# A graph layer's edge walk, from single edge rows in 16 slots to fours of rows in 32 slots

## The chip, the cores and the metric

One NeuronCore of one Trainium2 chip runs the whole program. The metric is the device time of one execution in microseconds (us), the median over several runs.

## What is computed

The reference normalizes 6250 nodes of 256 features, adds to them a mean over graph neighbours and a linear attention, and then a mixture of experts. The part that matters here is the neighbour sum over 100,000 edges, sorted by target node (`dst`); `src` is random.

```python
neigh_sum = jax.ops.segment_sum(input_matrix[src], dst, num_segments=N_NODES)
deg = jax.ops.segment_sum(jnp.ones_like(dst), dst, num_segments=N_NODES)
out = jax.nn.relu(concat([x, neigh_sum / max(deg, 1)]) @ W + b)      # GNN
qkv = rmsnorm(x) @ w_qkv
k = softmax(k, over all nodes); q = softmax(q, per head) * SCALE     # linear attention
out = rmsnorm((q @ (k.T @ v)) @ w_out + b_out) + x
x = x + top2_of_8_experts(layernorm(x))
```

## The kernel before

Nodes lie in 49 tiles of 128. Edges lie in rows of 128; 100,000 edges fill 782 rows, padded to 784. In the first stage layer norm is computed for all tiles, z = xn @ W_neigh is written to DRAM (`z_d`), and tables are made on the chip: for each step the row of edges that it takes (`srcT`, `dstT`) and the tile to which it adds (`acc_at`). A step is one row for one tile; a row that two tiles share has two steps. There are 832 steps in 104 blocks of 8 (`STEP_BLOCK`).

**The walk.** A step is four pieces of work on four engines. POOL gathers 128 rows of z (1 KB each) by an indirect DMA into one of 16 slots: a half of 8 slots is `G`, the other lies in `ring` (a part of `w2s`); line 677. DVE builds a 0/1 matrix S for four steps at once by comparing `iota` with `dstT` (`build_S`, line 1229). PE multiplies S of the step by the gathered rows into one of four PSUM banks (`walk` of the tensor block, line 1684; a product in float32 is two instructions in the profile). DVE adds the bank to the tile's accumulator at an address from a register (line 1245); eight registers are loaded at once at the head of a block (line 1234). The engines wait for one another by counting semaphores: POOL takes a group of four slots again when the four products of 16 steps before are signalled (`p_ready`); PE waits for the group's landing (`g_in`), for S (`s_built`), and for the addition four steps back (`acc_done`). `follow` (line 1673) is a filler product of PE after steps 3, 5 and 7 that nobody reads.

**What runs beside it.** The order of each engine is written out by hand, with hooks called after a given step of a block. Blocks 0 to 47 (here called stage A) carry keys and values of one tile each: ACT normalizes it (743), PE transposes it (1696), ACT copies it (862), SP stores it, PE multiplies (1703), ACT copies keys and values (866), DVE keeps the maximum (`kmax_tile`, 1276). Six blocks carry the context (1302, 885, 1724). The next 49 (stage B) carry the mixing of one tile each: SP loads the transposed tile, PE projects (`qu`, 1745), DVE does the first half of a softmax (`b_q1`, 1326 to 1330), ACT the exponential (893), DVE the second half (`b_q2`, 1334 to 1336), PE transposes q (`turn_q`, 1750), ACT copies it (907), PE multiplies (`mix_out`, 1755), DVE and ACT norm the tile before (`b_o1` 1340, 897 to 902, `b_o2` 1346 to 1349), SP stores it. Stage B also splits the second expert weights into two parts (`split_w2`, 440 and 441), and in tiles 16 to 23 sums bias products (`bfold` 1760, `b_fold` 1364). Then the last blocks run alone, and the router (group by group of up to 6 tiles, loads `load_ub` on SP) and the experts follow.

The hooks of stage B on PE: `qu` before the block, `turn_q` after step 5, `mix_out` after step 7. On DVE: `b_q1` after step 0, `b_o1` of the tile before after 1, `b_q2` after 3, `split_w2` after 5, `b_o2` of the tile before after 6.

The waits of POOL and of PE, in the code:

```python
until(pool, s["p_ready"], step - 2 * STEP_BLOCK + S_GROUP)
...
pe.wait_ge(g_in[half][k // S_GROUP], 16 * S_GROUP * (turn + 1))
pe.wait_ge(s["s_built"], 2 * i + k // S_GROUP + 1)
...
until(pe, s["acc_done"], step - 3)
```

## Time and profile before

| | |
|---|---|
| median of 3 runs (lowest, highest) | 2268.57 us (2268.07, 2277.15) |
| the profiled execution's span | 2267.2 us, 1.4 us below the median; the profile gives no other time of its own |
| PE, DVE, ACT, POOL busy | 74%, 58%, 40%, 52% of the span |
| walk, first gather to last addition | 90.5 to 1360 us |
| bytes moved | 325 MB, 143 GB/s on average |

The profile is one execution. Busy times are per engine; PEld is PE's weight load, which lies beside its products. "Idle before" is the time an engine stood before an instruction, with what ended it; "issue" names no releaser, and "remote" is a signal whose sender the trace doesn't name. The clock is PE's granted clock as a share of 2.4 GHz; 0.5 is 1.2 GHz. Line numbers are those of the kernel before. Tiles called `w2s_lent` and `edge_tabs_lent` are regions lent to several uses; `w2s_lent` is the slots of the second half in line 677.

### The profile page before, as it was taken

What the parts mean: (1) busy time and instruction counts of PE and PEld (TensorE: products, weight loads), DVE (VectorE), ACT (ScalarE), POOL (GpSimd) and SP (SyncE); (2) the same over time, 40 slices, a digit from 0 to 9 for tenths busy, and PEclk for the clock granted to TensorE, in tenths of its full rate; (3) what the DMA queues carried; (4) which work ended last, traced back from release to release, by engine and by line L of the source; (5) the groups of instructions that cost most, each with busy time, mean ns of one, the idle gap of its engine ahead of it and who ended that gap; (6) DMA issues with size and microseconds to landing.
All of it is one profiled execution on the core that took longest, in us unless ns stands there. A gap on an engine that the chain in (4) does not pass through costs nothing. (4 is left out here: it accounts for less than half of the span.)

```text
span 2267.2 us, 34877 instructions
## 1 busy us (share of the span) xinstructions
PE 1666.7 (74%) x9448; PEld 1326.2 (58%) x9449; DVE 1305.5 (58%) x3579; ACT 899.5 (40%) x1840; POOL 1177.1 (52%) x1203
## 2 busy tenths in 40 slices
PE   6656566665756666787666663555999999999997
PEld 5534343443434434434444342443999999999996
DVE  6434343443434557776777667753666666666663
ACT  6501010110110233333444336642666666666663
POOL 3466666666656666666666543663333333333333
PEclk9867777776768877889787885557999999999998
DMA  7433333333333465656666536745565565555554
GB/s 203 122 111 106 100 104 100 103 105 96 103 95 91 149 222 178 195 180 190 184 206 191 181 110 199 257 167 156 122 137 129 128 136 128 133 130 134 132 126 93
DMA packets 193411, 325.02 MB, mean 143 GB/s; under 512 B 34453, under 2 KB 136865, under 8 KB 192286
## 3 DMA queue, kind: packets, MB, share of 16 engines
q0 software_dynamic: 80912, 208.73, 35.0%
q1 hardware_dynamic: 103574, 112.56, 16.2%
q10 hardware_dynamic: 8824, 2.61, 0.6%
q8 instruction: 36, 0.59, 0.1%
q14 instruction: 65, 0.53, 0.1%
HBM read 244.30 MB, written 80.26 MB: 143 GB/s over the span
## 5 line engine op out<-in xcount | busy, mean ns | idle before, releaser
L1245 DVE TENSOR_TENSOR acc_lent<-acc_lent,bank 128x258 f32 x832 | 350.0, 421 | 527.5 <-remote 267.6
L677 POOL DMA_INDIRECT G<-z_d,edge_tabs_lent x416 | 404.3, 972 | 294.2 <-issue 119.6
L677 POOL DMA_INDIRECT w2s_lent<-z_d,edge_tabs_lent x416 | 402.0, 966 | 182.3 <-issue 117.8
L1684 PE MATMUL bank<-G,S_lent 128*128 128x258 f32 x832 | 286.0, 468 | 156.3 <-DVE acc_lent L1245 86.2
L1684 PE MATMUL bank<-w2s_lent 128*128 128x258 f32 x832 | 293.6, 478 | 114.7 <-issue 71.9
L1684 PEld LDWEIGHTS bank<-G,S_lent 128*128 128x128 f32 x832 | 166.8, 226 | 240.6 <-issue 167.7
L1684 PEld LDWEIGHTS bank<-w2s_lent 128*128 128x128 f32 x832 | 171.9, 233 | 203.0 <-issue 139.0
L717 POOL DMA_INDIRECT out_dram<-G,acc_lent x112 | 178.3, 1592 | 201.3 <-DVE G L1572 126.3
L1551 DVE TENSOR_TENSOR acc<-w1s,acc 128x512 fp32r<-128x512 f32 x224 | 155.0, 693 | 204.7 <-ACT acc L995 182.5
L1008 ACT ACTIVATE G<-bank,acc_lent 128x256 f32<-128x256 f32 x448 | 188.0, 471 | 195.6 <-DVE acc L1592 84.7
L1888 PE MATMUL bank<-w2s,acc 128*128 x896 | 261.5, 292 | 1.8 <-DMA edge_tabs<-w2lo_d 1.8
L1865 PE MATMUL bank<-acc 128*128 128x256 f32 x896 | 257.7, 288 | 3.4 <-DVE acc L1559 3.4
L1866 PE MATMUL bank<-acc 128*128 128x256 f32 x896 | 253.3, 283 | 0.0
L1867 PE MATMUL bank<-acc 128*128 128x256 f32 x896 | 253.3, 283 | 0.0
L1890 PE MATMUL bank<-w2s,acc 128*128 x896 | 251.5, 281 | 0.0
L866 ACT ACTIVATE w1s<-bank,r 128x256 f32<-128x256 f32 x49 | 23.2, 474 | 519.0 <-remote 332.6
L1865 PEld LDWEIGHTS bank<-acc 128*128 128x128 f32 x896 | 170.3, 190 | 3.9 <-issue 3.9
L1867 PEld LDWEIGHTS bank<-acc 128*128 128x128 f32 x896 | 170.9, 191 | 0.0
L1888 PEld LDWEIGHTS bank<-w2s,acc 128*128 128x128 f32 x896 | 169.7, 189 | 2.0 <-issue 2.0
L1866 PEld LDWEIGHTS bank<-acc 128*128 128x128 f32 x896 | 170.8, 191 | 0.0
L1890 PEld LDWEIGHTS bank<-w2s,acc 128*128 128x128 f32 x896 | 168.3, 188 | 0.0
L1592 DVE TENSOR_TENSOR acc<-G,acc 128x512 fp32r<-128x512 f32 x224 | 154.3, 689 | 7.0 <-ACT acc L1018 6.9
(294 smaller groups left out, 3134.6 us busy)
## 6 DMA issues: line engine op xcount, KB each, us to landing
S<-w2lo_d POOLq DMA_DIRECT2D x56, 512.0 KB
edge_tabs<-w2lo_d POOLq DMA_DIRECT2D x56, 512.0 KB
acc_lent<-bucket_d SPq DMA_DIRECT2D x56, 266.0 KB, 2.9
bu_d<-w2s_lent SPq DMA_DIRECT2D x98, 128.0 KB
w2s_lent<-bu_d SPq DMA_DIRECT2D x12, 768.0 KB
w1s<-in_L_ffn_W_dram SPq DMA_DIRECT2D x8, 1024.0 KB
w2s_lent<-in_L_ffn_W_dram SPq DMA_DIRECT2D x32, 256.0 KB
w2hi_d<-w2s_lent SPq DMA_DIRECT2D x32, 256.0 KB
```

Of the source, the lines that this page charges most:

```text
L677: pool.indirect_dma_start(out=G_half[half][:, k, 0:D], out_offset=None, in_=z_d[:, :], in_offset=bass.IndirectOffsetOnAxis(ap=srcT[:, step ...
L717: pool.indirect_dma_start(out=out[:, :], out_offset=bass.IndirectOffsetOnAxis(ap=nid[par][:, j:j + 1], axis=0), in_=ys[par][:, j, :], in_o ...
L1008: g = act.activation(raw[q % 2][:, k * MT:(k + 1) * MT], bank[q][:, k * MT:(k + 1) * MT], ACT.Gelu, bias=b1c[1 - par][:, 2 * q + k:2 * q + ...
L1245: dve.tensor_tensor(to, to, bank[k % 4][:, 0:ACCW], ALU.add).then_inc(s["acc_done"], 1)
L1551: dve.tensor_tensor(w1lo[:, :, cols].bitcast(F32R), w1_part(e, q), w1hi[:, :, cols], ALU.subtract).then_inc(s["w1_ready"], 1)
L1592: dve.tensor_tensor(hlo[:, cols].bitcast(F32R), raw[q % 2], hhi[:, cols], ALU.subtract).then_inc(s["h_split"], 1)
L1684: pe.matmul(bank[k % 4][:, 0:ACCW], S_half[half][:, k // S_GROUP, k % S_GROUP, :], G_half[half][:, k, :], start=True, stop=True).then_inc( ...
L1865: pe.matmul(to, hi, x_hi, start=(k == 0), stop=False)
L1866: pe.matmul(to, hi, x_lo, start=False, stop=False)
L1867: m = pe.matmul(to, lo, x_hi, start=False, stop=(k == DC - 1))
L1888: pe.matmul(to[j], hi, w_hi, start=False, stop=False, skip_group_check=True)
L1890: m = pe.matmul(to[j], lo, w_hi, start=False, stop=(c == HC - 1), skip_group_check=True)
```

## The change

The walk goes by turns in place of steps. A turn is one tile with a group of four rows (`QUAD`); there are 196 groups and at most 196 + 48 = 244 turns. The 32 slots (`RING` = 8 groups) all lie in `ring`; each row is gathered once, in order, and a group that two tiles share is used by two turns (or more) from the same slots. PE multiplies the four rows into one bank (start at the first, stop at the last), gives one signal, and issues a filler after every turn. DVE makes one addition a turn and builds S for the turn four ahead. Which slots a turn uses, which group it needs and when a group's slots are free depends on the data: three new tables (`base_at`, `need_at`, `free_at`) beside the accumulator's addresses are read into registers, eight at a time, by PE (two tables), POOL and DVE, and PE and POOL wait on those register values. POOL waits for the landing of group q-2 before it issues group q, and then signals it to PE by `quads_in`.

Stage A has two turns a tile, the context two turns a group, stage B three turns a tile for 37 tiles (`B_LONG`) and two for 12; one turn is left at the end. The tables are made in another way: source rows are transposed straight from the loaded edges, target rows come by two gathers of 128 groups in place of seven gathers of rows, and the accumulator's addresses no longer go through DRAM. Regions move: `w_kv`, `headmask`, `mkT`, `w_outs` to the rest of `G`, others to the end of `w2s`. On SP the load for router group 1 waits for the bias sum, and those for groups 2 and 3 for the last addition.

```diff
-STEPS_J = 7
-STEP_BLOCK = 8
-S_GROUP = 4
+QUAD = 4
+QUADS = EROWS // QUAD
+RING = 8
+IN_FLIGHT = 2
+DEPTH = 4
+REGS = 8
...
-BLOCKS = (EFULL + 1 + (NT - 1) + STEP_BLOCK - 1) // STEP_BLOCK
+TURNS = QUADS + NT - 1
+TURN_COLS = 248
...
+        RING_AT = 6 * D
+        RING_END = RING_AT + RING * QW_RING
+        taken = {"a": 0, "t": NT * KVW, "b": RING_END, "c": LATE}
...
+        S_of = [S[:, 0, :, :], S[:, 1, :, :]] + [G_flat[:, k * QUAD * P:(k + 1) * QUAD * P].rearrange("p (b n) -> p b n", n=P)
+                                                 for k in range(2)]
...
+        def groups_of(t):
+
+            if t < B_LONG:
+                return range(B_FIRST + 3 * t, B_FIRST + 3 * t + 3)
+            first = B_FIRST + 3 * B_LONG + 2 * (t - B_LONG)
+            return range(first, first + 2)
...
             load_ub(0)
+            sp.wait_ge(s["b1_mm"], 1)
             load_ub(1)
...
+            sp.wait_ge(s["acc_done"], TURNS)
             load_ub(2)
             load_ub(3)
...
-                pool.wait_ge(s["ecol_ready"], 1)
-                for j in range(STEPS_J):
-                    pool.indirect_dma_start(out=steps_e[:, j].rearrange("p k e -> p (k e)"), out_offset=None,
-                                            in_=edges_d.rearrange("r k e -> r (k e)"),
-                                            in_offset=bass.IndirectOffsetOnAxis(ap=ecol_i[:, j:j + 1], axis=0)
+                pool.wait_ge(s["qcol_ready"], 1)
+                for c in range(2):
+                    pool.indirect_dma_start(out=steps_i[:, c, :], out_offset=None,
+                                            in_=edges_d.rearrange("k (q r) e -> (k q) (r e)", r=QUAD),
+                                            in_offset=bass.IndirectOffsetOnAxis(ap=qcol_i[:, c:c + 1], axis=0)
...
-            pool.wait_ge(s["tables_ready"], 2)
+            pool.wait_ge(s["tables_ready"], 3)
             z_stored(pool)
-            for step in range(STEP_BLOCK * BLOCKS):
-                half, k = step // STEP_BLOCK % 2, step % STEP_BLOCK
-                if k % S_GROUP == 0:
-                    until(pool, s["p_ready"], step - 2 * STEP_BLOCK + S_GROUP)
-                    stand_alone(pool, s["waits_passed"])
-                pool.indirect_dma_start(out=G_half[half][:, k, 0:D], out_offset=None, in_=z_d[:, :],
-                                        in_offset=bass.IndirectOffsetOnAxis(ap=srcT[:, step:step + 1], axis=0)
-                                        ).then_inc(g_in[half][k // S_GROUP], 16)
+
+            def landed(q):
+
+                pool.wait_ge(g_in[q % IN_FLIGHT], 16 * QUAD * (q // IN_FLIGHT + 1))
+                pool.sem_inc(s["quads_in"], 1)
+            for q in range(QUADS):
+                if q >= RING:
+                    if q % REGS == 0:
+                        _, frees = nc.values_load_multi_w_load_instructions(
+                            rows_i[0:1, free_at + q:free_at + q + REGS], engines=[mybir.EngineType.Pool], min_val=1, max_val=TURNS)
+                    pool.wait_ge(s["p_ready"], frees[q % REGS])
+                if q >= IN_FLIGHT:
+                    landed(q - IN_FLIGHT)
+                for k in range(QUAD):
+                    row = QUAD * q + k
+                    pool.indirect_dma_start(out=ring_rows[:, row % (RING * QUAD), 0:D], out_offset=None, in_=z_d[:, :],
+                                            in_offset=bass.IndirectOffsetOnAxis(ap=srcT[:, row:row + 1], axis=0)
+                                            ).then_inc(g_in[q % IN_FLIGHT], 16)
+            for q in range(QUADS - IN_FLIGHT, QUADS):
+                landed(q)
...
+            def build_S(j):
+
+                dve.tensor_tensor(S_of[j % DEPTH], iota[:, :].rearrange("p (o n) -> p o n", o=1).to_broadcast([P, QUAD, P]),
+                                  dstT[:, QUAD * j:QUAD * (j + 1)].rearrange("p (g o) -> p g o", o=1).to_broadcast([P, QUAD, P]),
                                   ALU.is_equal).then_inc(s["s_built"], 1)
-
-            def walk(i, half, hooks={}):
-                _, places = nc.values_load_multi_w_load_instructions(
-                    acc_at[0:1, ds(STEP_BLOCK * i, STEP_BLOCK)], engines=[mybir.EngineType.DVE], min_val=0, max_val=NT * PAYW,
-                    skip_runtime_bounds_check_because="a count of at most NT tiles, times the width of one")
-                for k in range(STEP_BLOCK):
-                    step = STEP_BLOCK * i + k
-                    if k % S_GROUP == 0:
-                        until(dve, s["p_ready"], step - S_GROUP)
-                        build_S(2 * i + k // S_GROUP + 2, 1 - half, k // S_GROUP)
-                    dve.wait_ge(s["p_ready"], step + 1)
-                    until(dve, s["acc_done"], step)
-                    to = acc_flat[:, ds(places[k], ACCW)]
-                    dve.tensor_tensor(to, to, bank[k % 4][:, 0:ACCW], ALU.add).then_inc(s["acc_done"], 1)
-                    if k in hooks:
-                        hooks[k]()
-            build_S(0, 0, 0)
-            build_S(1, 0, 1)
+            places = {}
+
+            def turn(j):
+
+                if j % REGS == 0:
+                    _, loaded = nc.values_load_multi_w_load_instructions(
+                        rows_i[0:1, place_at + j:place_at + j + REGS], engines=[mybir.EngineType.DVE], min_val=0, max_val=NT * PAYW,
+                        skip_runtime_bounds_check_because="a count of at most NT tiles, times the width of one")
+                    places.update({j + k: v for k, v in enumerate(loaded)})
+                dve.wait_ge(s["p_ready"], j + 1)
+                until(dve, s["acc_done"], j)
+                to = acc_flat[:, ds(places[j], ACCW)]
+                dve.tensor_tensor(to, to, bank[j % DEPTH][:, 0:ACCW], ALU.add).then_inc(s["acc_done"], 1)
+                if j + DEPTH < TURNS:
+                    build_S(j + DEPTH)
+            for j in range(DEPTH):
+                build_S(j)
+            dve.memset(kmax, -3e38)
+            z_stored(dve)
+            dve.memset(ring_rows[:, :, D:ACCW], 1.0).then_inc(s["consts_dve"], 1)
...
+            for i in range(NT - 1):
+                turn(2 * i)
                 if i in late:
-                    hk[3] = late[i]
-                return hk
-            blocks(lambda i, h, turn: walk(i, h, a_hooks(i)), 0, NT - 1)
...
+            for t in range(NT):
+                mine = groups_of(t)
                 e = t - 16
-                hk[4] = lambda: (until(dve, s["bf_evac"], 2 * e), b_fold(e, 0))
-                hk[7] = lambda: b_fold(e, 1)
-                return hk
-            walk(B0, B0 % 2, b_hooks(0, True))
-            for first, end, hooks in ((1, SPLIT_AT + 1, b_hooks), (SPLIT_AT + 1, 16, with_split(b_hooks)), (16, 24, with_split(fold_hooks)),
-                                      (24, SPLIT_END + 1, with_split(b_hooks)), (SPLIT_END + 1, NT, b_hooks)):
-                blocks(lambda i, h, turn: walk(i, h, hooks(i - B0)), B0 + first, B0 + end)
-                if end == 24:
+                turn(mine[0])
+                b_q1(t)
+                if t:
+                    b_o1(t - 1)
+                turn(mine[1])
+                b_q2(t)
+                if 0 <= e < EXPERTS:
+                    until(dve, s["bf_evac"], 2 * e)
+                    b_fold(e, 0)
+                if len(mine) > 2:
+                    turn(mine[2])
+                if SPLIT_AT < t <= SPLIT_END:
+                    split_w2(t - SPLIT_AT - 1)
+                if t:
+                    b_o2(t - 1)
+                if 0 <= e < EXPERTS:
+                    b_fold(e, 1)
...
-            def walk(i, half, turn, hooks={}):
-                if -1 in hooks:
-                    hooks[-1]()
-                for k in range(STEP_BLOCK):
-                    step = STEP_BLOCK * i + k
-                    if k % S_GROUP == 0:
-                        pe.wait_ge(g_in[half][k // S_GROUP], 16 * S_GROUP * (turn + 1))
-                        pe.wait_ge(s["s_built"], 2 * i + k // S_GROUP + 1)
-                    until(pe, s["acc_done"], step - 3)
-                    pe.matmul(bank[k % 4][:, 0:ACCW], S_half[half][:, k // S_GROUP, k % S_GROUP, :], G_half[half][:, k, :], start=True, stop=True).then_inc(s["p_ready"], 1)
-                    if k in (3, 5, 7):
-                        follow()
-                    if k in hooks:
-                        hooks[k]()
-                        if k in (3, 7):
-                            follow()
+            bases, needs = {}, {}
+
+            def turn(j):
+
+                if j % REGS == 0:
+                    _, loaded = nc.values_load_multi_w_load_instructions(
+                        rows_i[0:1, base_at + j:base_at + j + REGS], engines=[mybir.EngineType.PE], min_val=0, max_val=(RING - 1) * QW_RING,
+                        skip_runtime_bounds_check_because="a slot of the ring, times the width of one")
+                    bases.update({j + k: v for k, v in enumerate(loaded)})
+                    _, loaded = nc.values_load_multi_w_load_instructions(
+                        rows_i[0:1, need_at + j:need_at + j + REGS], engines=[mybir.EngineType.PE], min_val=1, max_val=QUADS)
+                    needs.update({j + k: v for k, v in enumerate(loaded)})
+                pe.wait_ge(s["quads_in"], needs[j])
+                pe.wait_ge(s["s_built"], j + 1)
+                until(pe, s["acc_done"], j + 1 - DEPTH)
+                for k in range(QUAD):
+                    rows = ring[:, k * ACCW:(RING - 1) * QW_RING + (k + 1) * ACCW]
+                    m = pe.matmul(bank[j % DEPTH][:, 0:ACCW], S_of[j % DEPTH][:, k, :], rows[:, ds(bases[j], ACCW)],
+                                  start=(k == 0), stop=(k == QUAD - 1))
+                m.then_inc(s["p_ready"], 1)
+                follow()
...
+            for i in range(NT - 1):
+                turn(2 * i)
+                turn_a(i + 1)
+                turn(2 * i + 1)
+                kv(i)
...
+            for t in range(NT):
+                mine = groups_of(t)
                 e = t - 16
-                hk[3] = lambda: bfold(e, 0)
-                hk[6] = lambda: bfold(e, 1)
-                return hk
-            blocks(lambda i, h, turn: walk(i, h, turn, b_hooks(i - B0)), B0, B0 + 16)
-            pe.wait_ge(s["w1_in"], 16 * EXPERTS)
-            blocks(lambda i, h, turn: walk(i, h, turn, fold_hooks(i - B0)), B0 + 16, B0 + 24)
-            pe.wait_ge(s["bf_evac"], 2 * EXPERTS)
-            for c in range(HC):
-                m = pe.matmul(bank[5][:, c * EXPERTS:(c + 1) * EXPERTS], bacc[0:EXPERTS, c * P:(c + 1) * P], ident[0:EXPERTS, 0:EXPERTS],
-                              start=True, stop=True)
-            m.then_inc(s["b1_mm"], 1)
-            follow()
-            blocks(lambda i, h, turn: walk(i, h, turn, b_hooks(i - B0)), B0 + 24, B0 + NT)
-            walk(B0 + NT, (B0 + NT) % 2, (B0 + NT) // 2)
-            blocks(lambda i, h, turn: walk(i, h, turn), B0 + NT + 1, BLOCKS)
-            pe.wait_ge(s["acc_done"], STEP_BLOCK * BLOCKS)
+                if e == 0:
+                    pe.wait_ge(s["w1_in"], 16 * EXPERTS)
+                qu(t)
+                turn(mine[0])
+                if 0 <= e < EXPERTS:
+                    bfold(e, 0)
+                turn(mine[1])
+                turn_q(t)
+                if 0 <= e < EXPERTS:
+                    bfold(e, 1)
+                if len(mine) > 2:
+                    turn(mine[2])
+                mix_out(t)
...
+CTX_FIRST = 2 * (NT - 1)
+B_FIRST = CTX_FIRST + 12
+B_LONG = TURNS - 1 - B_FIRST - 2 * NT
```

## Rows read from the trace of the kernel before

**Rows 1.** Busy time by stretch: length, engines (instructions), clock, DMA share, GB/s.
```profile
0.00:90.50 90.50, 62.98 (x325) 51.46 (x326) 59.42 (x269) 65.99 (x146) 23.02 (x38) 0.98 0.65 177
90.50:669.00 578.50, 359.55 (x1204) 233.94 (x1204) 232.27 (x541) 59.52 (x145) 384.48 (x399) 0.73 0.36 103
669.00:750.00 81.00, 52.03 (x234) 38.04 (x235) 37.87 (x80) 8.31 (x10) 49.80 (x50) 0.77 0.29 86
750.00:1358.50 608.50, 421.88 (x1428) 254.03 (x1426) 418.37 (x1163) 222.10 (x405) 372.05 (x384) 0.82 0.60 183
```

**Rows 2.** Groups on POOL, 90 to 1358: busy and mean; idle before, by releaser.
```profile
L677 POOL DMA_INDIRECT G<-z_d,edge_tabs_lent x416 | 404.3, 972 | 294.2 <-issue 119.6 <-PE bank L1684 79.1 <-remote 69.2
L677 POOL DMA_INDIRECT w2s_lent<-z_d,edge_tabs_lent x416 | 402.0, 966 | 182.3 <-issue 117.8 <-PE bank L1684 41.5 <-remote 23.1
```

**Rows 3.** Timeline of POOL: start, length, instruction, idle before.
```profile
...
515.79 0.94 POOL L677 DMA_INDIRECT G<-z_d,edge_tabs_lent  x1 [0.30 <-issue]
517.04 0.94 POOL L677 DMA_INDIRECT G<-z_d,edge_tabs_lent  x1 [0.30 <-issue]
522.39 0.94 POOL L677 DMA_INDIRECT w2s_lent<-z_d,edge_tabs_lent  x1 [4.41 <-PE bank L1684]
```

**Rows 4.** Waits of DVE, 750 to 1358: total, times, longest.
```profile
DVE acc_lent L1245 <- remote: 86.3, 23, 7.0
```

**Rows 5.** Timeline, 804 to 825: products on PE, an addition on DVE.
```profile
804.44 1.93 PE L1684 MATMUL bank<-G,S_lent 128*128 128x258 f32 x4
...
817.34 1.91 PE L1684 MATMUL bank<-G,S_lent 128*128 128x258 f32 x8
...
824.22 0.42 DVE L1245 TENSOR_TENSOR acc_lent<-acc_lent,bank 128x258 f32 x1 [5.64 <-remote]
```

**Rows 6.** Timeline of DVE, 546.96: tile maximum and build of S.
```profile
546.96 0.29 DVE L1276 TENSOR_TENSOR w2s_lent<-w1s,w2s_lent 128x128 f32<-128x128 f32 x1
547.39 0.69 DVE L1229 TENSOR_TENSOR w2s_lent<-iota,edge_tabs_lent 128x512 f32<-128x512 f32 x1
```

**Rows 7.** Timeline at the first gather and the first product.
```profile
90.53 1.25 POOL L677 DMA_INDIRECT G<-z_d,edge_tabs_lent  x1 [26.29 <-DMA z_d<-w2s_lent]
...
97.39 2.95 PE L1684 MATMUL bank<-G,S_lent 128*128 128x258 f32 x6 [7.45 <-DMA G<-z_d,edge_tabs_lent]
```

**Rows 8.** Timeline between the context and the first mixing product.
```profile
741.86 0.22 PE L1673 MATMUL bank<-ones_b,before 128*128 128x128 bf16 x1
...
747.37 2.92 PE L1745 MATMUL bank<-w2s_lent,xTs 128*128 128x384 f32 x4 [0.46 <-DVE w2s_lent L1316]
```

**Rows 9.** Busy time of line 1684 alone by stretch: PE, PEld, clock.
```profile
90.50:669.00 578.50, 293.39 (x768) 156.75 (x768) 0.73 0.36 103
...
750.00:1358.50 608.50, 249.93 (x800) 161.56 (x799) 0.82 0.60 183
```

**Rows 10.** Timeline of DVE in a mixing tile: the two softmax parts.
```profile
803.29 0.28 DVE L1334 TENSOR_REDUCE small<-w2s_lent 128x4 f32<-128x128 f32 x1
...
803.82 0.29 DVE L1336 TENSOR_TENSOR w2s_lent<-w2s_lent,small 128x128 f32<-128x128 f32 x1
...
824.56 0.34 DVE L1326 TENSOR_SCALAR w2s_lent<-bank,r 128x128 f32<-128x128 f32 x1
...
825.47 0.42 DVE L1330 TENSOR_TENSOR w2s_lent<-bank,w2s_lent 128x256 f32<-128x256 f32 x1
```

**Rows 11.** Groups on PE, 750 to 1358: projection, output product, bias products.
```profile
L1745 PE MATMUL bank<-w2s_lent,xTs 128*128 128x384 f32 x193 | 93.8, 617 | 13.6 <-DMA xTs<-xnT_d 9.3 <-issue 4.2
...
L1755 PE MATMUL bank<-w2s_lent 128*128 128x256 f32 x98 | 44.1, 542 | 19.1 <-issue 9.9 <-ACT w2s_lent L907 9.2
L1760 PE MATMUL bank<-w1s,small 128*8 128x512 f32 x64 | 34.6, 668 | 7.8 <-issue 5.7 <-DVE w2s_lent L1364 2.1
```

**Rows 12.** Busy time of two stretches: granted clock.
```profile
804.00:808.00 4.00, 3.83 (x10) 2.69 (x11) 3.48 (x11) 2.41 (x5) 2.11 (x3) 0.50 0.29 87
815.00:819.00 4.00, 3.96 (x18) 2.71 (x17) 3.01 (x8) 1.34 (x2) 3.08 (x4) 1.00 0.52 166
```

361 lines of the change are left out of this document (196 added, 165 removed).

## The prediction, made before the changed kernel was timed

> **What bounds the kernel now.** I read the busy time by stage first. The span has five parts: layer norm and tables to 90.5 us; the edge walk beside the keys and values (stage A) to 669; the walk beside the context to 750; the walk beside the mixing of 49 tiles (stage B) to 1358.5; then the router and the experts, which the change leaves alone [rows 1]. So the change plays in 90.5 to 1358.5, 1268 us.
>
> In the walk no engine is full: POOL is busy for two thirds, PE for 62 to 69% with the clock at 0.73 to 0.82 [rows 1]. The groups of POOL say why. A gather takes 0.969 us and 0.30 us pass before the next; 832 of them are 806.3 us busy and 476.5 us idle, 26.3 of that before the first [rows 2, 3]. With 0.30 each, 250 us of the idle time belong to the issue, and about 200 us are waits for a free slot: 832 x 1.27 = 1057 of the 1256 us that the gathers spread over. One such wait: eight issues at 1.25 us, then 4.41 us until products of the half before are signalled [rows 3]. The walk has 16 slots, and a group of four is asked for again 12 gathers (15.2 us) after it was issued.
>
> Behind that wait stands a slow handshake, not work. In stage B DVE waited 23 times, 86.3 us in all and up to 7.0, before additions for which the trace names no releaser [rows 4]. In one of them PE runs eight product instructions (two to a product, so four products) from 817.34 in 1.91 us, and the first addition of these comes at 824.22, after 5.64 us of waiting [rows 5]. Every step passes one product PE to DVE and one bank back, 832 times, with four banks between them.
>
> **The change, part by part.**
>
> *Gathers.* 784 instead of 832, since a row that two tiles share is fetched once: 784 x 1.27 = 995.7 us instead of 1057, so -61 us on POOL. POOL gains a read of eight registers per eight groups of four (24 in all). On DVE the same read costs nothing that shows: the tile maximum starts at 546.96 (0.29 long), the build behind it at 547.39 [rows 6]. POOL issues nothing meanwhile, so 0 from below and, from above, the 1.25 us of one gather; I take 0.5, nearer to DVE's row since it is the same instruction: 12 us (ends 0 and 30). The two waits and one increment per group I price at nothing; today's wait and increment leave the 1.25 us rhythm intact [rows 3]. Ceiling for them: 0.3 us, one issue gap, x 196 = 59 us.
>
> *The wait added on POOL.* Before group q it waits for the landing of q-2, whose last gather was issued 4 x 1.25 us earlier. The first four gathers start at 90.53 and PE starts at 97.39, that is at most 2.8 us after the fourth started (94.3) plus rounding [rows 7]. So it waits for nothing, with 2 us to spare; queued behind it are all gathers. It makes each group visible to PE only 8 gathers (10.2 us) after its start: +3.3 us once, at the first product.
>
> *32 slots.* A group's place is asked for again 28 gathers (35.6 us) after its last issue; less the late landing signal some 25 us are left for PE and DVE, against 15.2 now. The handshake stalls of 5 to 6 us fit in. The slot waits, about 200 us, go wherever PE and DVE keep up on average.
>
> *Stage A and context under POOL's pace.* From the reference's edges, turn 96 takes group 87 and turn 107 group 96. Group 87 is signalled at 90.5 + 89 x 4 x 1.27 = 543, group 96 at 588. With 6 us of register reads and 5.5 us for the serial end of the context as now (last context products 741.9, first mixing product 747.37 [rows 8]), and some 10 us for lost coupling, stage B begins at 610 instead of 750: **-140 us**. PE must keep up: stage A's 384 products cost 293.4 us, 0.76 each at that clock [rows 9]; four are 3.06 us, with filler 3.3; 96 turns are 317 us and the rest of PE's work there 66 us more (359.6 - 293.4 [rows 1, 9]), 383 of about 455 us. It fits.
>
> *Additions.* 244 instead of 832, 588 x 0.42 = 247 us off DVE; builds of S go from 208 to 244 at 0.69, +25 us [rows 5, 6]. DVE was 40 and 69% busy [rows 1], so this pays only inside handshakes.
>
> *Products.* 976 instead of 832. In stage B a tile has 12 (three turns) for 37 tiles and 8 (two turns) for 12, instead of 8. This is the cost. PE takes its orders in sequence, and the turn of q sits between turns 2 and 3, after DVE's second softmax part, which sits after the second addition. Worked out for a three-turn tile, with the clock high: q/u projection 1.6, turn 1.9, turn 1.9 (8 instructions 1.91 [rows 5]): PE at 5.4. DVE has turn 1's signal at 3.8, adds and builds (1.1) to 4.9, first softmax part 1.33 (824.56 to 825.89) to 6.2, earlier output 0.4, addition and build to 7.7, second part 0.82 (803.29 to 804.11) to 8.5 [rows 10]. PE turns q to 8.8, third turn to 10.7, output product 0.5: 11.2 us. At the present mean prices (projection 93.8/49 = 1.91, turn 4 x 249.9/400 = 2.50 plus 0.25, output 0.9 [rows 9, 11]) the same sum is 13.7. A two-turn tile ends by the same DVE path at 10 and 11.7. Eight tiles carry the bias products, 34.6 us in all [rows 11], of which I count 20.
> Which clock? The bounds are 0.82, today's in stage B, and 0.98, the first stage's [rows 1]. PE's idle piece before the turn of q is 2 to 3 us, shorter than the 5 us pieces that go; I take the middle, 0.9: 12.1 and 10.7 us. Stage B = 37 x 12.1 + 12 x 10.7 + 20 = 596 us, against 608.5 now: **-12 us**. POOL would allow 37 x 11.4 + 12 x 6.9 = 505, so here PE's sequence takes over as the bound, the ring stays full and POOL waits again, at no cost.
>
> *Moved on SP.* The loads for router groups 2 and 3 now wait for the last addition too; they come behind the landing of the last store as it is, and DVE makes its last addition beside that store: nothing, at most one turn (2 us) if the order turns round. The load of router group 1 waits for the bias sum of tile 23 but is issued after tile 41: nothing. The tables (two gathers instead of seven, two DMAs fewer on SP, other small DVE work) lie beside the stores of z, for which POOL waits 26.29 us before the walk [rows 7]: nothing; that is 26 us of cover.
>
> **Sum.** -140 - 12 + 3 = -149 us. The page's span is 2267.2 us, 1.4 us below the median of 2268.6; the forecast is 2268.6 - 149, **2120 us**.
>
> **The clock, row against rule.** At a granted 0.50 (804 to 808) four product instructions take 1.93 us; at 1.00 (815 to 819) eight take 1.91 [rows 5, 12]: 1.2 and 2.4 GHz, a factor of two on every product. The Trainium skill, page "TensorE: Matmul & The Clock Gate", section "HAM oscillation — how this bites in real kernels", says that a TensorE which waits between bursts falls back to half clock and starts each burst cold. The trace agrees as far as the walk's 0.73 to 0.82 goes; taken strictly, the rule would put all of stage B at half clock, the second rival below.
>
> **Rivals.**
> 1. *PE stays at full clock in stage B.* 37 x 11.2 + 12 x 10 + 20 = 554 us, -55: **2077 us**. For it: 0.98 in the first stage. Against: each stretch of the walk is far below it. Chance 0.17. POOL's own floor, stage B at 505, would be 2030.
> 2. *Slower: PE falls to 1.2 GHz in stage B.* The place is the wait before the turn of q, in every tile. All at half clock (projection 2.92, four products 3.86 and a filler 0.3 [rows 5, 8]), a three-turn tile is 2.9 + 4.2 + 4.2 for PE, DVE's path to 13.5, then 0.5 + 4.2 + 1.2 = 19.4 us, a two-turn tile 15; with the bias work 720 + 180 + 40 = 940 us, +330 against now, less 140: 2460. It decides from a mean of 15 us per tile, a clock of about 0.72. Stage A's 0.73 speaks for it; against, PE has fewer and shorter idle pieces than now. The form to expect is 15.5 us a tile, 760 + 20 us, +172 less 137: **2303 us**. Chance 0.08.
> 3. *The late signals stay.* The 86.3 us [rows 4] come on top of the 596: **2206 us**. For it: the trace doesn't tell why PE's signals come late. Against: there are 3 handovers for 8. Chance 0.13.
> 4. *Stage A is not at POOL's pace* because keys, values and norms pass through ACT and back in each tile: 10.5 instead of 9.5 us, +48: **2168 us**. Chance 0.12.
> 5. *It does less than it says*: the slots are not what POOL waited for, and only the 61 us of gathers are saved, 2207 us. Against: the 4.41 us wait is on products of the half before [rows 3]. Chance 0.04.
>
> **Numbers.** Forecast 0.46. The range runs from between POOL's floor and rival 1 to just above rivals 3 and 5: 2045 to 2215. It leaves out rival 2 and the far ends of the others, 0.17 together; the open prices (register reads 0 to 30, waits 0 to 59, both only where POOL sets the pace) lie inside. A difference of 0.5% is what a measurement of this kernel can tell from none, 11 us: slower 0.08 (rival 2), same 0.02, faster 0.90.
>
> **What would show it.** Right: gathers at 1.27 us without slot waits until about 600 us; stage B beginning near 610; tiles of about 12 us with PE's idle time before the turn of q; POOL idle on products only in stage B; clock near 0.9 there. Wrong: slot waits in stage A (rivals 4, 5), idle time of 5 us before additions (rival 3), a clock of 0.75 or less in stage B (rival 2).

## The result: slower, 2346.6 us against 2268.3

The changed kernel takes 2346.6 us in the median (2339.18 to 2355.51, 4 runs), the kernel before 2268.3; the ratio is 1.035 with a 95% interval of 1.029 to 1.040. The forecast was 2120 us with a range up to 2215. The profiled execution has a span of 2337.4 us, 70.2 more than before.

The profile after, busy time by stretch (columns: length; PE, PEld, DVE, ACT, POOL busy with instructions; clock; DMA share; GB/s). The lines answer to [rows 1]: keys and values, and the mixing.

```profile
90.90:643.00 552.10, 302.15 (x1165) 235.38 (x1166) 116.21 (x263) 61.78 (x148) 372.78 (x380) 0.76 0.37 105
705.00:1426.00 721.00, 483.70 (x1651) 327.87 (x1649) 340.23 (x934) 221.68 (x402) 363.51 (x365) 0.83 0.50 151
```

The first projection of the mixing starts at 706.0 us (before 747.4, forecast 610) and the last addition at 1425.2 (before 1360.0). So 41.4 us are won before the mixing, 106.5 lost in it (719.2 against 612.7) and 5.1 behind the last addition: +70.2 from span to span.

Groups on PE in the mixing (columns as in [rows 11]), and PE's waits in stage A (total, times, longest):

```profile
L1761 PE MATMUL bank<-w2s_lent,S_lent 128*128 x544 | 161.6, 450 | 54.2 <-issue 51.7 <-DVE G L1280 1.6 <-DVE acc_lent L1295 0.8
L1830 PE MATMUL bank<-ident,w2s_lent 128*128 128x128 f32 x49 | 18.9, 385 | 161.5 <-DVE w2s_lent L1391 118.0 <-issue 37.6 <-DVE S_lent L1280 3.4
```

```profile
PE bank L1770 <- ACT w2s_lent L753: 90.0, 11, 30.9
PE bank L1770 <- issue: 52.3, 9, 19.8
PE bank L1761 <- issue: 39.4, 10, 6.2
```

Three things are to be seen. PE stood 161.5 us before the turns of q, 118.0 of them for DVE's second softmax part. It stood 51.7 us before products with no releaser in the profile. And in stage A it waited up to 30.9 us at a stretch for ACT's norm. The timeline there:

```profile
108.16 2.00 PE L1761 MATMUL bank<-w2s_lent,G 128*128 x8 [1.96 <-POOLq L674]
...
120.37 1.14 PE L1777 MATMUL bank<-G,xTs 128*128 128x256 f32 x4
121.35 1.91 PE L1761 MATMUL bank<-w2s_lent,S_lent 128*128 x8
...
136.85 0.42 DVE L1295 TENSOR_TENSOR acc_lent<-acc_lent,bank 128x258 f32 x1 [21.00 <-remote]
...
152.94 0.47 ACT L877 ACTIVATE w1s<-bank,r 128x256 f32<-128x256 f32 x1 [36.66 <-remote]
152.97 0.42 DVE L1295 TENSOR_TENSOR acc_lent<-acc_lent,bank 128x258 f32 x1 [15.10 <-remote]
...
154.23 0.69 PE L1770 MATMUL bank<-ident,w2s_lent 128*128 128x128 f32 x2 [30.92 <-ACT w2s_lent L753]
```

The product of turn 2 ends at 110.2 and its addition starts at 136.85; the keys and values of 120.37 are copied at 152.94. PE can't run on meanwhile, since its next transpose waits for ACT, and ACT for PE's signal. Call a turn late when its addition starts over 1 us after the recorded end of its products: 57 of the 108 turns ahead of the mixing are late, 528.6 us in sum, up to 32.5; in the mixing 26 of 136, 92.5 us.

```profile
L1749 PEldq TENSOR_LOAD <-w2s_lent x31: 1929/1934/3258, 92.2 to 1401.4; - x31
```

```profile
L1753 PEldq FUSED_REGOPS  x248: 146/146/156, 96.5 to 1407.7; - x124
L1753 PEldq SEQ_ASSERT  x248: 18/18/18, 96.7 to 1407.9; - x124
L1753 PEldq TENSOR_LOAD <-w2s_lent x31: 1927/1932/2829, 94.3 to 1403.6; - x31
```

So each eighth turn PE's sequencer does two reads of 1.93 us and eight checks of bounds. The prediction has neither. In the walk of the kernel before only DVE has such a read, and it took 0.60 us:

```profile
L1234 DVEq TENSOR_LOAD <-w2s_lent x104: 593/597/936, 89.7 to 1353.1; - x104
```

### The profile page after: what moved, and what is told of

It is laid out like the page before. It is cut to its first block and busy times, and to the rows that moved or that the text cites. A ratio compares the mean times of both kernels' runs of the same rounds, so it can differ in the third digit from the quotient of the medians.

```text
span 2337.4 us, 35331 instructions
## 1 busy us (share of the span) xinstructions
PE 1665.0 (71%) x9622; PEld 1401.9 (60%) x9623; DVE 1094.3 (47%) x3020; ACT 900.4 (39%) x1840; POOL 1143.1 (49%) x1150
## 5 line engine op out<-in xcount | busy, mean ns | idle before, releaser
L685 POOL DMA_INDIRECT w2s_lent<-z_d,edge_tabs_lent x784 | 776.5, 990 | 536.2 <-issue 257.2
L1295 DVE TENSOR_TENSOR acc_lent<-acc_lent,bank 128x258 f32 x244 | 103.0, 422 | 765.7 <-PE bank L1761 400.5
L1761 PE MATMUL bank<-w2s_lent,S_lent 128*128 x976 | 301.1, 464 | 105.3 <-issue 95.6
L1761 PEld LDWEIGHTS bank<-w2s_lent,S_lent 128*128 128x128 f32 x976 | 219.6, 234 | 172.1 <-issue 130.1
L1761 PE MATMUL bank<-w2s_lent,G 128*128 x976 | 274.3, 432 | 2.0 <-POOLq L674 2.0
L1761 PEld LDWEIGHTS bank<-w2s_lent,G 128*128 128x128 f32 x976 | 206.8, 219 | 55.5 <-issue 15.5
L904 ACT ACTIVATE w2s_lent<-w2s_lent 128x128 f32<-128x128 f32 x49 | 15.2, 310 | 430.2 <-DVE w2s_lent L1383 352.8
L1770 PE MATMUL bank<-ident,w2s_lent 128*128 128x128 f32 x98 | 26.3, 361 | 201.4 <-ACT w2s_lent L753 90.0
```

The source lines that it names most:

```text
L685: pool.indirect_dma_start(out=ring_rows[:, row % (RING * QUAD), 0:D], out_offset=None, in_=z_d[:, :], in_offset=bass.IndirectOffsetOnAxis( ...
L1295: dve.tensor_tensor(to, to, bank[j % DEPTH][:, 0:ACCW], ALU.add).then_inc(s["acc_done"], 1)
L1761: m = pe.matmul(bank[j % DEPTH][:, 0:ACCW], S_of[j % DEPTH][:, k, :], rows[:, ds(bases[j], ACCW)], start=(k == 0), stop=(k == QUAD - 1))
L1770: m = pe.transpose(bank[5][:, c * P:(c + 1) * P], xr[:, c * P:(c + 1) * P], ident[:, :])
```

## Two conditions

The experiments were run in six series (a, c, e, g, h, i), each with runs of the kernel before beside them. That kernel took 2063 to 2069 us in four series (a, c, e, h) and 2266 to 2278 in two (g, i), as at first. In the first four hardly a turn is late ahead of the mixing; in the other two, as at first, many are. The ratio is always within a series; where runs of two series are compared below, both are named. Runs without a ratio are single executions. Times in us; "mixing from" is the first projection, "last" the last addition, "late" the late turns ahead of the mixing:

```
label                      time     before  ratio (95%)               mixing from  last     late
a1_no_gathers              2036.5   2068.7                            480.3        1150.1   0
a2_quarter_rows            2153.4   2068.7                            584.7        1266.8   0
a3_pool_on_additions       2194.5   2068.7                            616.2        1304.5   0
a4_two_products            2126.1   2068.7                            611.6        1234.5   4
c1_before                  2071.6   2063.0                            655.3        1185.9
c2_after                   2197.5   2063.0  1.063 (1.056 to 1.070)    620.0        1309.5   0
c3_constants_on_pe         2122.9   2063.0  1.029 (1.027 to 1.030)    606.9        1236.9   1
c4_constant_needs          2131.3   2063.0  1.034 (1.032 to 1.036)    605.6        1238.4   1
e1_turn_q_later            2141.1   2064.4  1.037 (1.034 to 1.039)    613.6        1245.4   0
e2_later_and_constants     2081.4   2064.4  1.008 (1.005 to 1.010)    607.8        1189.9   0
e3_ring_of_16              2195.7   2064.4                            614.4        1309.4   0
g1_aligned                 2314.7   2266.0  1.023 (1.019 to 1.026)    715.5        1410.2   58
g2_aligned_later           2250.4   2266.0  0.992 (0.990 to 0.995)    704.3        1327.5   66
h1_no_gathers              2035.6   2064.2                            479.1        1149.4   0
h2_aligned                 2123.2   2064.2  1.028 (1.023 to 1.032)    607.1        1235.7   0
h3_aligned_later           2048.8   2064.2  0.990 (0.987 to 0.994)    602.4        1158.8   0
i1_no_gathers              2081.1   2278.0                            493.3        1164.4   4
i2_before                  2275.1   2278.0                            751.2        1362.0
```

What late signals cost each kernel comes out of one profiled execution in either condition, by stretch. The kernel before (first profile against c1) takes 92.1 us more up to the mixing, 82.1 in it and 23.4 behind the last addition (907.2 against 883.8), 197.5 in all. The changed kernel (first profile against c2) takes 86.0, 29.7 and 27.8 more, 143.5 in all. So late signals cost the changed kernel much less in the mixing than the kernel before, and nearly as much ahead of it.

## Experiments a: gathers, products, waiting engines

In a1, only the first ring is gathered and the later groups are signalled at once.

```diff
-                for k in range(QUAD):
+                for k in range(QUAD if q < RING else 0):
```

> Leaves out: all gathers of rows after the first 32 (groups 0 to 7); the later groups are signalled at once and their products use the old rows. Everything else, 244 turns included, stays. In the changed kernel 57 of the 108 turns before the mixing have their addition over 1 us after the recorded end of their products (528.6 us in all, up to 32.5), and the mixing starts at 706 us. Theory G (the gathers are what holds PE's signals back): no turn is late by over 1 us, stage A falls to PE's own work, about 96 turns x 3.6 us = 350 us, so that mixing starts near 500 us and the whole takes about 2030 us. Theory P (the lateness is PE's own, in bursts after idle time, whatever POOL does): some 50 late turns before the mixing as now, mixing starts at 650 us or later, the whole above 2230 us.

In a2 each gather after the first 32 fills 32 rows; in a3 POOL waits for additions; in a4 a turn has two products.

```diff
-                    pool.indirect_dma_start(out=ring_rows[:, row % (RING * QUAD), 0:D], out_offset=None, in_=z_d[:, :],
-                                            in_offset=bass.IndirectOffsetOnAxis(ap=srcT[:, row:row + 1], axis=0)
+                    pool.indirect_dma_start(out=ring_rows[0:P if q < RING else 32, row % (RING * QUAD), 0:D], out_offset=None, in_=z_d[:, :],
+                                            in_offset=bass.IndirectOffsetOnAxis(ap=srcT[0:P if q < RING else 32, row:row + 1], axis=0)
...
-                    pool.wait_ge(s["p_ready"], frees[q % REGS])
+                    pool.wait_ge(s["acc_done"], frees[q % REGS])
...
-                for k in range(QUAD):
+                for k in range(QUAD // 2):
```

> Leaves out: of each gather after the first 32, three quarters of its 128 rows (only 32 partitions are filled anew), so a quarter of the packets and bytes; the number of gathers and of signals stays 784. Theory G in the form that packets or bytes are what counts: late turns before the mixing fall from 57 to under 15, and mixing starts near 600 us or earlier. Theory G in the form that each gather instruction counts, whatever its length: between 40 and 57 late turns, start of the mixing near 690. Theory P: 57 late turns, 706 us.

> Nothing left out. POOL waits for the additions (acc_done) in place of PE's signal p_ready, so that p_ready has one waiting engine, DVE, in place of two. Theory W (a signal that two engines wait for, one against a register, is what comes late): under 10 late turns, mixing starts near 610 us, the whole about 2200 us. Theories G and P: nothing changes by over 1%, 2325 to 2370 us, since an addition ends 0.4 us after the signal.

> Leaves out: the third and fourth product of each turn, so 4 product instructions in place of 8; gathers, builds, additions and waits stay. Theory P in the form that the number of PE's instructions in a burst decides (signals lag once some 40 to 60 of them have gone through): about half as many late turns, 25 to 30, and 250 us of lateness before the mixing. Theory G: late turns stay at 45 to 60, for the gathers are as before, and the time falls only by PE's work in the mixing, 74 turns x 0.96 us + 74 x 0.5, some 100 us.

Measured: times as in the table, and hardly a late turn in any, because in this series signals were on time: the kernel before was 200 us faster too. a1's numbers are theory G's (no late turn, mixing from 480.3 us, 2036.5 in all), but where nothing is late without the edit either they prove nothing; so of the expectations on lateness none is decided here, and theory W was not tried again where signals are late; a3's time stands at 2194.5 where the unaltered changed kernel takes 2197.5 in c2, no difference. a2 reaches the mixing at 584.7 us, 31.5 before a3, since its shorter gathers take 896 ns up to there, against 990 in c2. One thing a1 does show: without gathers the mixing still takes 669.8 us, against 689.5 in c2, so in the mixing the gathers hardly bound the changed kernel. What a4 shows of the price of products where signals are on time is a lower bound: three-turn tiles take 12.14 us with six products less per tile, against 13.46 in c2, but the granted clock in the mixing is 0.77 there, against 0.84 in c2.

## Experiments c: both kernels where signals are on time, and the reads

c1 is the kernel before and c2 the changed kernel, unaltered. c3 replaces both of PE's reads by constants worked out from the edges, c4 the second read only.

```diff
-                if j % REGS == 0:
-                    _, loaded = nc.values_load_multi_w_load_instructions(
-                        rows_i[0:1, base_at + j:base_at + j + REGS], engines=[mybir.EngineType.PE], min_val=0, max_val=(RING - 1) * QW_RING,
...
-                    _, loaded = nc.values_load_multi_w_load_instructions(
-                        rows_i[0:1, need_at + j:need_at + j + REGS], engines=[mybir.EngineType.PE], min_val=1, max_val=QUADS)
...
+                bases[j], needs[j] = GROUP_OF[j] % RING * QW_RING, GROUP_OF[j] + 1
```

> The kernel before, word for word, for its profile on the chip of this call: in a1 to a4 the kernel before took 2068.7 us, 200 less than the 2268.3 measured first, and no turn of the changed kernel's variants was late. Theory S (late signals of PE belong to some chips, and both kernels have them there and only there): where the whole is near 2070, the additions follow the products within 0.5 us unless DVE is busy, gathers run at 1.27 us apart without slot waits before the mixing, and mixing starts near 610 us; where the whole is near 2268, the picture is that of the first profile (mixing from 747 us).

> The changed kernel, word for word, timed beside the kernel before on this chip. Theory S with theory R (register reads on PE): on a chip without late signals the changed kernel gains nothing before the mixing, where both go at POOL's pace, and loses about 8 us per 8 turns in the mixing: 2195 us against 2069, a ratio of 1.06. If the change's 32 slots still pay before the mixing on such a chip, the ratio is 1.02 or less.

> Leaves out: PE's reads of its two tables into registers (slot and needed group of each turn); both are written into the kernel as constants worked out from the edges. Nothing else changes. In a3 PE's sequencer takes 6.46 us for one pair of reads of eight registers (664.68 to 671.14: 1.94 and 2.12 for the two loads and 2.3 for eight checks of their bounds), tiles with such a read last 17.5 to 20 us and the others 10.2 to 13. Theory R: stage B loses 17 such reads, 17 x 8 = 136 us, and the whole takes about 2060 us, with no tile of the mixing over 14 us outside the bias tiles. Theory D (stage B is bound by the chain of DVE's softmax parts and its 12 products a tile, and reads lie beside waits): gain under 40 us.

> Leaves out: the read of the second table (the needed group, with the checks of bounds) only, constants in its place; the slot is still read, 1.94 us per eight turns. Theory R: 4.5 of the 6.46 us go and the clock stays up, so at least two thirds of c3's gain, about 90 to 110 us. Theory D: under 30 us.

Busy time by stretch, up to the mixing and in it. Of c1, the kernel before:

```profile
88.00:655.00 567.00, 381.51 (x1434) 282.26 (x1434) 272.82 (x621) 68.38 (x155) 432.41 (x441) 0.83 0.40 116
655.00:1186.00 531.00, 393.32 (x1431) 243.55 (x1431) 418.96 (x1170) 221.40 (x405) 388.98 (x392) 0.89 0.69 212
```

Of c2, the changed kernel:

```profile
88.00:620.00 532.00, 359.54 (x1377) 268.82 (x1377) 140.44 (x303) 68.42 (x155) 400.99 (x405) 0.83 0.40 115
620.00:1310.00 690.00, 482.21 (x1648) 326.74 (x1648) 339.25 (x933) 221.17 (x401) 377.18 (x380) 0.84 0.52 161
```

Of c3, with constants:

```profile
607.00:1237.00 630.00, 460.81 (x1648) 315.13 (x1648) 339.52 (x932) 221.23 (x401) 384.73 (x390) 0.87 0.58 178
```

Neither expectation on the stretch before the mixing held. c1 begins the mixing at 655.3 us, not near 610, with gathers 1.31 us apart and 38.5 us of slot waits in the whole walk; and c2 does win there, where it was expected to win nothing. Its ratio of 1.063 is the one expected.

Between c1 and c2: 35.3 us are won before the mixing, 158.9 lost in it (689.5 against 530.6). Of these 158.9, c3 gives back 59.5 (630.0), and 13.1 more before the mixing: PE's reads cost 74.6 us of the whole (2197.5 less 2122.9). That is between theory R, which had 136, and theory D with under 40: I had put down whole slow tiles to the reads, and part of their length remains as waits before the turn of q, which grow by 20.6 us (112.1 in c2, 132.7 in c3). c4 shows that the second read with its checks is nearly all of it, 66.2 us. Why the first read costs so little isn't shown; it may lie beside the projection that PE is still working on. One pair in c2:

```profile
666.90 1.45 PE L1825 MATMUL bank<-w2s_lent,xTs 128*128 128x384 f32 x4
672.70 3.81 PE L1761 MATMUL bank<-w2s_lent,S_lent 128*128 x8 [4.35 <-issue]
...
684.99 1.91 PE L1761 MATMUL bank<-w2s_lent,G 128*128 x8
```

After 4.35 us without a product the eight instructions take 3.81 us, at a granted clock of 0.50 (1.2 GHz), where they take 1.91 at 1.00 further on: the read costs its time once on the sequencer and up to 1.9 us again through the clock. Behind 13 of the 17 pairs of reads in the mixing of c2 the eight instructions take 3.6 to 3.8 us.

The other 99 us are in the groups on PE in the mixing. In c1:

```profile
L1684 PE MATMUL bank<-w2s_lent 128*128 128x258 f32 x400 | 120.0, 430 | 30.3 <-DMA w2s_lent<-z_d,edge_tabs_lent 17.2 <-DVE acc_lent L1245 13.0
L1684 PE MATMUL bank<-G,S_lent 128*128 128x258 f32 x400 | 116.2, 419 | 28.1 <-DMA G<-z_d,edge_tabs_lent 15.5 <-DVE acc_lent L1245 12.4
...
L1750 PE MATMUL bank<-ident,w2s_lent 128*128 128x128 f32 x49 | 17.6, 360 | 43.0 <-DVE w2s_lent L1336 43.0
```

And in c3:

```profile
L1755 PE MATMUL bank<-w2s_lent,S_lent 128*128 128x258 f32 x544 | 149.7, 425 | 7.1 <-POOLq L674 7.1
L1755 PE MATMUL bank<-w2s_lent,G 128*128 128x258 f32 x544 | 148.8, 423 | 4.1 <-POOLq L674 4.1
...
L1824 PE MATMUL bank<-ident,w2s_lent 128*128 128x128 f32 x49 | 17.6, 360 | 132.7 <-DVE w2s_lent L1391 132.7
```

Products +62 us (298.5 against 236.2), the wait before the turn of q +90 (132.7 against 43.0), waits before products -47 (11.2 against 58.4); the other groups make up the rest. The kernel before was at POOL's pace here too: its 832 gathers start over 1088 us, 1.31 us each. The change made PE's sequence the bound in its place. Mean tiles, from projection to projection (tile 36, the last with three turns, isn't counted; with it c2 has 13.6):

```
                     three turns (28)   with bias products (8)   two turns (11)
c1 (the same tiles)  10.36              11.31                    10.58
c2                   13.46              18.88                    11.94
c3                   12.18              16.46                    11.91
h2                   12.07              16.85                    11.46
h3                   11.33              13.23                    10.27
```

## Experiments e: PE's order, and the ring

e1 turns q one projection later, e2 does so with constants; e3 halves the ring.

```diff
                 qu(t)
+                if t:
+                    turn_q(t - 1)
                 turn(mine[0])
+                if t:
+                    mix_out(t - 1)
...
-                turn_q(t)
...
-                mix_out(t)
```

```diff
-RING = 8
+RING = 4
```

> Nothing left out. Only PE's order in the mixing changes: the turn of q of tile t comes after the projection of tile t+1, its output product after that tile's first turn (before: turn of q after the second turn of its own tile). On the chips of the last two calls PE waits 112 us in the mixing before the turn of q (49 waits, at most 2.9). Theory R plus waits: those 112 us go, except where the reads of registers (17 x 6.5 us in the mixing) or POOL (1.27 us a gather) take over: stage B about 690 - 90 = 600 us, the whole about 2105 us where the kernel before takes 2063, ratio about 1.02. Rival: the wait moves to the first turn of the next tile or to a late addition, gain under 30 us, ratio over 1.045.

> Leaves out: PE's reads of its tables, constants in their place, as in c3; and PE's order of e1. Theory: with neither reads nor the wait before the turn of q a three-turn tile is PE's own work, 1.6 + 5.8 + 1.2 + fillers = about 9.5 us, a two-turn tile about 8, so POOL's pace (1.27 us a gather) bounds nearly all of the walk: mixing from 607 us, last addition near 1150, the whole about 2035 us, 1.3% below the kernel before at 2063. Rival: DVE's chain (additions, builds, softmax parts) bounds at 10.5 to 11 us a tile as in the kernel before: 2065 to 2085 us.

> Nothing left out. The ring is 16 slots (4 groups) in place of 32, all else as in the changed kernel (POOL reads its table by fours). Where signals are not late (kernel before near 2063): theory S says that the slots beyond 16 pay nothing before the mixing, start within 10 us of 620; PE and DVE hold a group for about two turns. Rival: with waits for a landing two groups back and turns that share groups, 16 slots are too few, and the mixing starts later than 680 us. Where signals are late (kernel before near 2268): mixing later than the 706 us of the changed kernel by 50 us or more.

e1 gains 56 us over c2 where 92 were expected, e2 41 over c3 where 88 were. e2's 2081.4 lies in its rival's range of 2065 to 2085, though its three-turn tiles take 11.5 us and not 10.5 to 11. The wait before the turn of q is gone (3.5 us in e1), but half of it came back elsewhere. PE's waits in the mixing of e1:

```profile
PE bank L1761 <- issue: 63.7, 13, 6.4
PE bank L1825 <- DMA xTs<-xnT_d: 61.9, 18, 14.3
...
PE bank L1830 <- DVE w2s_lent L1391: 3.5, 5, 1.6
```

The load of the next transposed tile stands on SP behind the store of the tile before, which waits for DVE's last piece; that piece now comes later. This is only part of it: in h3, where that piece comes earlier again, 47.2 of the 61.9 us are left. e3 takes 2195.7 us with mixing from 614.4: with 16 slots the changed kernel does what it does with 32. Where signals are on time the added slots pay nothing.

## Experiments g and h: the address of the tables

The four tables begin 8 bytes past a multiple of 32 bytes, since a region of 130 words lies ahead of them. g1 swaps the two; nothing else changes:

```diff
-        mv1 = lend("b", HID + 2)[0:MEM]
         rows_f = lend("b", 4 * 2 * P)[0:1, :]
         rows_i = rows_f.bitcast(I32)
+        mv1 = lend("b", HID + 2)[0:MEM]
```

g2 adds e1's order, puts DVE's `b_o2(t - 1)` ahead of the third turn, and PE's second bias product behind it. h2 and h3 are the same two kernels where signals are on time.

> Nothing left out. The region of the four tables moves by 130 words, so that each read of eight registers begins at a multiple of 32 bytes, as the kernel before's reads did; in the changed kernel they begin 8 bytes off one (word 14282 and on). There a read of eight takes 1.93 us on PE and 1.84 on DVE and POOL (0.94 for four in e3), in the kernel before 0.60. Theory A (the address makes the read slow): 0.6 us a read, so PE's pair with its checks falls from 6.46 to about 3.8 us, and the whole by 17 x 2.7 to 17 x 4 (clock), 45 to 70 us, to 2125 to 2150 us where the kernel before takes 2063. Rival: the reads are slow for another reason (the loop, the engine): still 1.9 us, no change in the time (2190 to 2200).

> Nothing left out. The aligned tables of g1; PE's order of e1 (turn of q after the next projection, output product after the next tile's first turn); DVE finishes the tile before (b_o2) before the third turn instead of after it, so that SP comes free earlier for the load of the transposed tile, for which PE waits 62 to 68 us in e1 and e2; the second bias product goes after the third turn. From e1's 2141: less 45 for the reads, less 40 to 60 for SP and the bias tiles: 2040 us, 1.2% under the kernel before at 2063. Rival: the load of the transposed tile is late because its own transfer takes over 5 us, not because SP is late: 2080 to 2095 us, slower than before.

> The kernel of g1 again. Where signals are late: g1's 2314.7 us, ratio 1.022. Where they aren't (kernel before near 2063): theory A gives 2197 less 45 to 70, that is 2130 to 2150 us, with three-turn tiles outside the bias tiles at 12.7 us on average (13.46 in c2, 12.18 with constants in c3).

> The kernel of g2 again. Where signals are late: g2's 2250 us, ratio 0.992. Where they aren't: 2035 to 2055 us, ratio 0.985 to 0.996, with POOL's pace as the bound before the mixing (from 610 us) and tiles of 10.5 us in it; if the three-turn tiles stay over 11.2 us there, the ratio is over 1.0.

The read in h2, against 1927/1935/3753 in c2:

```profile
L1753 PEldq TENSOR_LOAD <-w2s_lent x31: 587/589/1033, 92.0 to 1210.5; - x31
```

Theory A holds: the move of the tables by 130 words alone makes the read 0.59 or 1.93 us. h2 takes 2123.2 us, slightly less than forecast (2130 to 2150) and as much as c3 gave with no read at all: what is left, 1.2 us of reads and 2.3 of checks per pair, costs nothing that shows beside c3. Where signals are late g1 gives 2314.7, 32 us under the changed kernel of the first measurement.

g2 and h3 are faster than both kernels, though by under 1% of the kernel before: 0.992 (0.990 to 0.995) and 0.990 (0.987 to 0.994) of the kernel before. In h3 the mixing takes 556.4 us, 26 more than in c1, and the 53 us won before it (602.4 against 655.3) outweigh that. The bias tiles fall from 16.85 to 13.23 us. Three-turn tiles stay at 11.33, over my bound of 11.2, and the kernel is faster than before all the same.

## Experiments h1, i1 and i2: what late signals need

> The kernel of a1 again (leaves out all gathers after the first 32), for a chip on which signals come late (the kernel before near 2266 us). Theory G (the gathers hold PE's signals back): no late turn there either, mixing from 480 us as in a1. Theory P (the lateness is PE's own on such a chip): 40 or more late turns before the mixing, mixing from 550 us or later. On a chip where the kernel before takes 2063 it repeats a1 (2036) and tells nothing of this.

> The kernel of a1 and h1 a third time, for a chip on which signals come late (the kernel before near 2266 us). Theory G: no late turn, mixing from 480 us, the whole near 2036. Theory P: 40 or more late turns before the mixing, mixing from 550 us or later, the whole above 2150. Where the kernel before takes 2063 it tells nothing of this.

> The kernel before, for its profile on the chip of this call. Where it is near 2266: mixing from about 747 us, as in the first profile. Where it is near 2063: mixing from 655 us, as in c1.

h1 repeats a1 where signals are on time, and tells nothing of this. i1 is the run that decides: in its series the kernel before takes 2278, mixing from 751.2 us (i2), and without gathers the changed one takes 2081.1 with four late turns. Its gathers and its late additions:

```profile
L686 POOL DMA_INDIRECT w2s_lent<-z_d,edge_tabs_lent x32 | 31.1, 972 | 43.0 <-issue 43.0
```

```profile
109.64 0.42 DVE L1296 TENSOR_TENSOR acc_lent<-acc_lent,bank 128x258 f32 x1 [6.07 <-remote]
...
136.32 0.42 DVE L1296 TENSOR_TENSOR acc_lent<-acc_lent,bank 128x258 f32 x1 [17.56 <-remote]
```

The 32 gathers start from 90.9 to 130.5 us. Turns 1 to 4 are late, up to 25.6 us, with additions from 109.6 to 138.4; after that no turn ahead of the mixing is late, and two in it are by 1.1. So late signals in the walk need POOL's gathers, and theory P, which puts them down to PE alone, falls. It is one execution, and theory G had no late turn and 2036 us where there are four and 2081.1.

The traces hold a second witness. i1 takes 44.6 us more than a1, the same kernel, and 30.2 of these come behind the last addition, all in the router, where neither kernel gathers rows of z; the experts take the same time in both. There POOL writes rows by 98 indirect DMAs, and DVE waits for products of PE (`rank_mm`). First POOL in i1, then that wait in i1 and in a1:

```profile
L700 POOL DMA_INDIRECT bucket_d<-acc_lent,edge_tabs_lent x98 | 99.3, 1013 | 90.0 <-issue 50.3 <-DVE acc_lent L1545 39.6
...
DVE small L1527 <- remote: 43.0, 6, 10.0
...
DVE small L1527 <- PE bank L1902: 3.3, 7, 0.8
```

The kernel before has the same wait in the router: 42.8 us in i2, 3.2 in c1. So it is not the walk's gathers in particular: in these traces signals of PE come late where POOL issues one indirect DMA after another, in the walk and in the router. The link in the router is read from the traces and not tested by an edit.

What makes the same program have late signals in some series and not in others stays open: the number of the chip doesn't tell (it is 3 in both c and i). Nor was it shown whether packets, bytes or the number of gathers count, since in series a, where a2 tried it, signals were on time.

## Why the prediction was wrong

**The two failures in numbers.** The profiled execution is 216.9 us above c3, which has no reads on PE and signals on time. Reads on PE make up 73.4 of these (c2 less c3, by span) and late signals 143.5 (first profile less c2). The kernel without reads wasn't run where signals are late, so the split assumes that the two add up. The forecast had neither term: the first was not in its list, the second it let the ring swallow. That c3's 2122.9 us is the forecast of 2120 is partly luck: its mixing takes 34 us more than forecast, and the part behind the last addition 23.6 less than in the trace that the forecast started from.

**Gathers and register reads.** The step that failed first is the list itself: it prices a read of eight registers on POOL and on DVE and none on PE, which has two every eight turns, with checks. I had followed the wait and the address into PE's code and not the reads that feed them. Measured: 74.6 us (c2 less c3, medians). The size was wrong as well. I took a read as costing nothing on DVE, by a gap in [rows 6], and 1.25 us at most on POOL; in the changed kernel it is 1.93 us on PE and at least 1.84 on DVE and 1.83 on POOL, for a reason that no row of before shows, the tables' new address. The 61 us of gathers were right as far as they could be seen: 35.3 us earlier at the mixing in c2, 48 in c3, the reads between them.

**32 slots.** "The handshake stalls of 5 to 6 us fit in." They did not stay at 5 to 6: with larger turns the lateness came in pieces of up to 32.5 us, and in stage A it doesn't act through the ring, but through PE, ACT and back: at 706 us POOL has issued 420 gathers, where the turns so far took 388, so all 32 slots ahead are filled. That is rival 4's path, with rival 3's cause. Mixing began at 706 us instead of 610, 96 us late, where rival 4 had 48. Where signals are on time the step is exact, 606.9 to 620.0 against 610, but there the kernel before has few slot waits to lose (38.5 us in c1), and 16 slots do as well (e3).

**Stage A's -140.** Its basis, that the 200 us of slot waits are a matter of slots, is true of neither condition. They were POOL's share of the late signals, which 32 slots don't cure (41 us won); where signals are on time only 38.5 us of them are there (c1).

**Products and tiles in the mixing.** The working holds for a three-turn tile where signals are on time: 12.1 forecast, 12.18 and 12.07 measured without the costly reads, with the wait before the turn of q at 2.7 us (132.7/49; forecast 2 to 3) and the clock at 0.87 to 0.90 (forecast 0.9). Mis-sized are the two-turn tiles, 11.9 for 10.7, and the bias tiles, 4.3 us each over a plain one, 34 us for 20. Together 630 us against 596. What failed is the comparison: 596 was set against 608.5, while the kernel before needs 530.6 where signals are on time: some 78 of the 608.5 belong to late signals, which the change doesn't touch. The reads add 59.5 us to the 630 (c2) and late signals 29.7 more: 719.2.

**Additions, landing wait, moved loads.** As forecast nothing shows. POOL's landing wait and increments leave the gathers 1.25 us apart; the part behind the last addition is 884.4 us in c2 against 883.8 in c1 (912.2 against 907.2 in the first profiles).

**Rivals.** Rival 2 named the right side, the right stage and nearly the size for its tiles (15.5 us; three-turn tiles took 14.87), and the wrong mechanism: the clock in the mixing was 0.83, not 0.72. Rival 3 named the cause and put it in the wrong place: it priced late signals at 86.3 us in the mixing and nothing before it. They cost 29.7 us in the mixing, where DVE's waits with a "remote" releaser are 56.7 us, and 86.0 before it, where I let the ring swallow them. Where two rivals and a term left out add up, a range built from one rival at a time is too narrow. As for the Trainium skill's page "TensorE: Matmul & The Clock Gate", section "HAM oscillation — how this bites in real kernels": that a waiting TensorE starts its next burst cold is what c2 shows (3.81 us after the 4.35 us wait, 1.91 later). The whole mixing ran at 0.83 to 0.90, so the strict reading that the prediction gave the page, every burst cold, doesn't hold here.

## What to carry to other kernels

List for every engine every instruction that a change gives its sequencer, reads of registers and their checks among them, before pricing any. If a step saves an engine from waiting, ask what the wait is made of, and measure it once with its suspected source taken away. A table that is read into registers in an inner loop is worth starting at a multiple of 32 bytes: against a start 8 bytes past one that gave 74 us where signals were on time (h2 against c2) and 32 where they were late (g1 against the first measurement). Other offsets were not tried for reads of eight. Before a difference of a few per cent is explained, time both kernels in more than one series: here the same kernel before took 2063 or 2268 us.
